# Where the keys of an adjacency tile are shifted: from VectorE to ScalarE, three steps ahead

## What is computed

```
src = concatenate([_s, _d, loop]);  dst = concatenate([_d, _s, loop])
order = argsort(dst);  src = src[order];  dst = dst[order]

def gin_conv(x, src, dst, eps, W1, ln_g, ln_b, W2):
    agg = segment_sum(x[src], dst, num_segments=n)
    h = (1.0 + eps) * x + agg
    h = relu(layer_norm(h @ W1, ln_g, ln_b))
    return h @ W2

xn = layernorm(x)
x = x + gnn_0(xn, edge_index) + mix_0(xn)
x = x + ffn_0(layernorm(x))
xn = layernorm(x)
x = x + gnn_1(xn, edge_index) + mix_1(xn)
x = x + ffn_1(layernorm(x))
```

## Time and profile before

| | us |
|---|---|
| median of 3 runs | 2361.12 (2360.05 to 2365.64) |
| the profiled execution's own time | 2366.88 |
| its span, first to last instruction | 2365.1 |
| the stage of `build_adjacency`, first compare to last | 155.0 to 473.2 |

### The profile page before, as it was taken

One profiled execution on the slowest core, in us unless ns is written; L12 is line 12 of the kernel. 1 busy time (PEld: TensorE's weight loads), 2 busy tenths in 40 slices (PEclk: granted clock), 3 DMA queues, 4 the chain that ended last, 5 costly groups with the idle time before them and its releaser, 6 DMA issues. The chain is left out here.

```text
span 2365.1 us, 41463 instructions
## 1 busy us (share of the span) xinstructions
PE 1997.1 (84%) x12047; PEld 1624.9 (69%) x12047; DVE 1474.2 (62%) x3791; ACT 1036.3 (44%) x1835; POOL 551.5 (23%) x612
## 2 busy tenths in 40 slices
PE   6938888878877758998697898769999965999998
PEld 3526666656633447998365776569888854999997
DVE  3479999978832655554565322399999656444443
ACT  3525555545511524665351343166666430333332
POOL 1000000047611734554310000000000001454443
PEclk9979999977898559999798999989999956999999
DMA  2014334330077301221502342212121081633332
GB/s 69 0 46 133 117 121 129 109 93 1 1 168 211 103 25 54 71 71 54 127 0 54 95 136 63 56 42 65 53 66 53 0 291 54 195 79 75 49 47 33
DMA packets 90653, 189.74 MB, mean 80 GB/s; under 512 B 14121, under 2 KB 58432, under 8 KB 90570
## 3 DMA queue, kind: packets, MB, share of 16 engines
q1 hardware_dynamic: 72906, 157.31, 23.0%
q0 software_dynamic: 17664, 31.47, 6.4%
HBM read 124.22 MB, written 64.52 MB: 80 GB/s over the span
## 5 line engine op out<-in xcount | busy, mean ns | idle before, releaser
L2224 PEld LDWEIGHTS experts_ps_h<-experts_xt,experts_up 128*128 128x128 f32 x2944 | 351.8, 194 | 10.3 <-issue 3.3
L2224 PE MATMUL experts_ps_h<-experts_xt,experts_up 128*128 128x128 f32 x2944 | 353.0, 277 | 3.0 <-DVE experts_xt L2346 1.8
L2851 PE MATMUL gat_ps_o<-Y,gat_prob_t 125*125 125x256 f32 x1250 | 273.9, 379 | 0.0
L2851 PEld LDWEIGHTS gat_ps_o<-Y,gat_prob_t 125*125 125x125 f32 x1250 | 232.7, 188 | 33.7
L1233 PE MATMUL adj_ps_w<-adj_one_k,adj_one_s 128*125 128x500 bf16 x1000 | 178.8, 305 | 78.6 <-DVE adj_one_k L1164 56.0
L2236 PE MATMUL experts_ps_o<-experts_down,experts_hid 128*128 128x256 f32 x960 | 226.7, 379 | 0.0
L2284 ACT ACTIVATE experts_down<-down 128x1024 f32 (+1 forms) x120 | 138.8, 1157 | 175.7 <-DVE experts_out L2334 77.1
L2316 DVE COPY experts_up<-up 128x1024 f32 (+1 forms) x184 | 123.1, 698 | 112.8 <-issue 68.8
L1233 PEld LDWEIGHTS adj_ps_w<-adj_one_k,adj_one_s 128*125 128x125 bf16 x1000 | 98.3, 138 | 128.6 <-DVE adj_one_k L1164 60.2
L2236 PEld LDWEIGHTS experts_ps_o<-experts_down,experts_hid 128*128 128x128 f32 x960 | 173.2, 190 | 18.7
L1177 ACT ACTIVATE adj_tile<-adj_ps_w 125x500 bf16<-125x500 f32 x250 | 95.8, 438 | 150.1 <-PE adj_ps_w L1233 150.1
(11 more groups left out here) (436 smaller groups left out, 3783.9 us busy)
## 6 DMA issues: line engine op xcount, KB each, us to landing
adjacency<-adj_tile SPq DMA_DIRECT2D x25, 683.6 KB
adjacency_t<-adj_tile_t SPq DMA_DIRECT2D x25, 683.6 KB
adj_in<-adjacency_t SPq DMA_DIRECT2D x25, 683.6 KB
QT<-adjacency SPq DMA_DIRECT2D x25, 683.6 KB
cnt<-adjacency_t SPq DMA_DIRECT2D x25, 683.6 KB
up<-in_L_ffn_w SPq DMA_DIRECT2D x32, 512.0 KB, 6.3
down<-in_L_ffn_w SPq DMA_DIRECT2D x16, 512.0 KB, 7.1
up<-in_L_ffn_W SPq DMA_DIRECT2D x8, 512.0 KB, 6.2
```

The source lines that it names most:

```text
L2224: last = nc.tensor.matmul(ps[:, h * 128:(h + 1) * 128], w[:, k * H + h * 128:k * H + (h + 1) * 128], xt[b][:, k, :], start=(k == 0), stop= ...
L2851: last = nc.tensor.matmul(ps_o[b][0:ROWS, 0:C], prob_t[:, s * ROWS:(s + 1) * ROWS], K.Y[:, s, :], start=(s == 0), stop=(s == TILES - 1))
```

## The change

ScalarE makes `key_here`. After the copies of each step it loads the first chunk of the step three ahead from `table` into a register and runs one activation (identity with a bias) that adds the negative of that step's first key (`win_neg`, a new table of GpSimd) to the keys of the four chunks. The first three are made before its first copy. `key_here` has five buffers in place of two, one for each step of a tile. VectorE's instruction goes; its compares still wait for `keyed`, which ScalarE now raises. `table` has three further entries, zero, for the steps beyond the last, ahead of the number of further chunks.

```
-        table = m.sb("table", (1, WINS + 1), I32)
+        table = m.sb("table", (1, WINS + 4), I32)
-        win_key = m.sb("win_key", (CH, WINS))
+        win_key, win_neg = m.sb("win_key", (CH, WINS)), m.sb("win_neg", (CH, WINS + 3))
-        key_here = [m.sb(f"key_here{i}", (CH, FIXED)) for i in range(2)]
+        key_here = [m.sb(f"key_here{w}", (CH, FIXED)) for w in range(WPT)]
...
+            nc.gpsimd.iota(win_neg[:], [[-WIN * TILES, WINS + 3]], base=0, channel_multiplier=0,
+                           allow_small_or_imprecise_dtypes=True)
...
-            v.tensor_copy(table[:, WINS:WINS + 1], most_chunks[:]).then_inc(table_ready, 1)
+            v.memset(table[:, WINS:WINS + 3], 0)
+            v.tensor_copy(table[:, WINS + 3:WINS + 4], most_chunks[:]).then_inc(table_ready, 1)
...
                     dve.wait_ge(win_done, win + 1 + START)
-                    v.tensor_scalar(key_here[half][:], key_all[:, bass.ds(first, FIXED)],
-                                    win_key[:, bass.ds(win, 1)], None, ALU.subtract).then_inc(keyed, 1)
                     v.tensor_tensor(one_s[half][:], K.number_row[:, None, 0:ROWS].to_broadcast((CH, FIXED, ROWS)),
...
                     dve.wait_ge(keyed, win + 1 + START)
                     for j in range(FIXED):
-                        v.tensor_scalar(one_k[half][:, j, :], key_row[:], key_here[half][:, j:j + 1], None,
+                        v.tensor_scalar(one_k[half][:, j, :], key_row[:], key_here[w][:, j:j + 1], None,
                                         ALU.is_equal).then_inc(one_ready, 1)
...
+            def keys(t, w):
+                win = t * WPT + w
+                first = act.value_load(table[:, bass.ds(win, 1)], min_val=0, max_val=CHUNKS)
+                nc.scalar.activation(key_here[w][:], key_all[:, bass.ds(first, FIXED)], ACT.Identity,
+                                     bias=win_neg[:, bass.ds(win, 1)]).then_inc(keyed, 1)
+
             def window(t, b, w):
...
                 last.then_inc(win_read, 1)
+                if w < 2:
+                    keys(t, w + 3)
+                else:
+                    keys(t + 1, w - 2)
...
+            act.wait_ge(table_ready, 1 + START)
+            for w in range(3):
+                keys(0, w)
             for w in range(WPT):
                 window(0, 0, w)
```

More of the change, by code:

```diff
@@ L1140, in _ @@
             dve.drain()
-            v.tensor_copy(table[:, WINS:WINS + 1], most_chunks[:]).then_inc(table_ready, 1)
+            v.memset(table[:, WINS:WINS + 3], 0)
+            v.tensor_copy(table[:, WINS + 3:WINS + 4], most_chunks[:]).then_inc(table_ready, 1)
             dve.wait_ge(table_ready, 1 + START)
-            more = dve.value_load(table[:, WINS:WINS + 1], min_val=1, max_val=MORE_MAX)
+            more = dve.value_load(table[:, WINS + 3:WINS + 4], min_val=1, max_val=MORE_MAX)
             def tile(t, b, i):
@@ L1228, in _ @@
             pe.wait_ge(table_ready, 1 + START)
-            more = pe.value_load(table[:, WINS:WINS + 1], min_val=1, max_val=MORE_MAX)
+            more = pe.value_load(table[:, WINS + 3:WINS + 4], min_val=1, max_val=MORE_MAX)
             def add(banks, ones, keys, start, stop):
```

## The result

The change takes 2337.72 us (median of 4 runs, 2335.93 to 2338.82), against 2361.78 for the kernel before in the same series: a ratio of 0.9892, with a 95% interval of 0.9875 to 0.9910. It is 24 us faster, three times what was forecast, and lies under the range. The profiled execution took 2337.41 us, its span is 2335.7.

A forecast was written before the change was run, and what follows sets the result against it. VectorE was taken as the bound. 24 tiles at 0.32 us give 7.7; with the first tile's 0.65, less 0.1, 8.2 us come off 2361.1: 2352.9, rounded to 2353, range 2345 to 2362.

The forecast's parts named there:

- The bound before: In the changed stage VectorE was taken as nearly full, busy 115.48 of 120 us, with ScalarE half idle.
- The subtraction's 0.13 per step: Taking the subtraction off VectorE saves 0.13 us per step, 0.65 per tile; an undisturbed stride falls from 2.41 to 2.28.
- The load: VectorE's register load of the coming step's chunk stays behind `one_s`, meets the stores' DMA elsewhere; 0.20 of 0.65 per tile left.
- 0.35 + 0.1 per tile: Losses in us claimed for a tile's two long register loads on VectorE, first and second, each growing under a store.
- the subtraction's 16.3 us: Rival: the whole saving on VectorE comes through, 0.65 by 25 tiles, 16.3 us, giving 2345; chance 0.17.
- the prediction's own signs of being wrong: Loads staying short, calm stride not falling, or TensorE's wait for ScalarE well above 0.94 and for VectorE gone.
- The length of the first long load: VectorE's load after a tile's first store starts 0.39 us earlier, becomes 1.2 us long, losing 0.35 per tile.
- The second load: VectorE's load after a tile's other store comes 0.17 us earlier, grows to 1.37, losing 0.04 to 0.14, taken as 0.1.
- ScalarE's part: Load and activation per step are free in the mean, but delay the copy after the fourth step's by 0.3 us.
- The rival in which ScalarE makes the kernel slower: ScalarE's load holds the fifth copy, the TensorE and ScalarE ring passes 12.83; a 2.0 us load gives 2373.6; chance 0.08.
- VectorE's new period still decides: VectorE's period per tile, 12.83 - 0.32 = 12.51 us, stays above the 12.2 of TensorE with ScalarE.
- their ring: TensorE's cycle with ScalarE per tile: 12.83 - 0.93 = 11.90 us, with 0.3 of delay 12.2.

The follow-up runs named there:

- e5_parity_before: The kernel before, with the PSUM set chosen by the step's running number instead of its place in the tile: 2363.46 us, ratio 1.0003.
- e2_both: The change with VectorE's subtraction and its wait put back, ScalarE still making keys that nothing reads: 2363.11 us, ratio 1.0000 to the kernel before.
- e9_own_wait: The change, with each step's first compare also waiting for the count VectorE's own `more_k` raises, no engine work added: 2349.32 us, ratio 0.9937 to the kernel before.
- e6_parity_after: The change, with the PSUM set chosen by the step's running number: 2331.49 us, ratio 0.9863 to the kernel before.
- e4_noload: The kernel before, without VectorE's register loads for the second and third step of each tile (counts wrong): 2350.13 us, ratio 0.9943.
- e10_early_sub: The kernel before, with VectorE's subtraction moved ahead of `more_s` instead of behind `more_k`: 2360.69 us, ratio 0.9981.
- e3_ahead: The change, with ScalarE's key behind the fourth step's copies issued ahead of them: 2334.49 us, ratio 0.9892 to the kernel before.
- e8_spare_sub: The change, with VectorE also subtracting into a tile nobody reads, without a semaphore: 2353.67 us, ratio 0.9968 to the kernel before.

## Why the prediction was wrong

**The bound before: right.** VectorE set the pace (`e5_parity_before`, `e2_both`).

**The subtraction's 0.13 per step: right.** The calm stride was forecast at 2.28 and is 2.28.

**The load: this step failed.** "The stride from `one_s` to the next `more_s` keeps its parts, the load among them." The load's start, 0.26 us after `one_s`, was taken for a fixed part of the step. It was the effect of the wait that the subtraction carried, and it went with it. `e9_own_wait` puts a wait back and gets the forecast's case: two long strides per tile, a period of 12.4 in the mean where 12.51 was forecast. So 0.35 + 0.1 per tile were booked as lost on top of the 0.65 that the loads cost before, and instead that 0.65 left the path too: where VectorE sets the pace its lead covers the first load (`e6_parity_after`), where it doesn't the loss lies beside TensorE's wait, and the second load is short. No case was priced with the loads cheaper than before (a second load ahead of the reading was named, but without the 0.53 us that it saves), so the lower end of the range was the subtraction's 16.3 us; `e4_noload` measures what was missing there, 15.4 us of the stage. Of the prediction's own signs of being wrong the last came: TensorE's wait for VectorE's compares is gone, and that for ScalarE's copies rose, to 1.14.

The length of the first long load came out as forecast (1.2 us; 1.12 to 1.17 from the sixth tile on), but by luck. The load was to start 1.6 us after the store's issue and to end 2.85 after it, where the DMA's reading was thought to end. In the tile shown it starts 1.1 us after the issue at 294.02 and ends 2.2 after it, while the DMA engines read on (share 0.91 in 296.40 to 297.00, below). The assumed end held where the load starts later: 304.64 is the issue in `e10_early_sub`, and the load from 306.1 ends 2.8 us after it.

The second load was to reach 1.37 us. In the change, from the sixth tile to the last but one, it takes 0.30 in every other tile and 0.62 to 1.04 in the rest, for two reasons. VectorE is further ahead of the second store than was thought: the load starts 0.8 us after the issue instead of 1.6, which alone makes it 0.63 to 1.10 (`e3_ahead`). And where ScalarE's late copy holds the store back by a further 0.35 us, the load starts some 0.4 us after the issue and is short; the load of the fourth step then takes 0.6 to 0.7 us and costs nothing. The second effect was named in the prediction, at 0 to 0.5 per tile, and taken at 0.12.

**ScalarE's part: mechanism right, sizes off.** The fifth copy is late behind the key, in the five tiles shown by 0.04 to 0.07 us in one and 0.33 to 0.35 in the next (the waits less 0.94), 0.2 in the mean against 0.3 forecast. The activation of 128x4 takes 0.30 us, not 0.2:

```profile
L1175 ACT ACTIVATE adj_key_here<-adj_key,adj_win_neg 128x4 f32 x128 | 38.3, 299 | 67.0 <-issue 38.5 <-DVE adj_table L1144 28.4
```

The rival in which ScalarE makes the kernel slower needed loads over 1.48 us; the longest is 1.396.

**"VectorE's new period still decides": wrong,** and it follows from the load. TensorE and ScalarE decide, at 11.79; their ring was forecast at 12.2. Of the 0.4 between, 0.3 was TensorE's time at the third step, counted as its own where it had followed VectorE's compares, and 0.1 is ScalarE's smaller delay.

## What to carry to other kernels

A wait on an engine's own earlier instruction can be a wait of its sequencer, as it was here: look at what stands behind it (a register load, an address) and at whether the start of that follows the wait. When an edit takes such a wait away, give the work behind it a case in which it becomes free, not only those in which it stays or grows. And once the bound moves, try again what was worth nothing: the choice of PSUM banks gave 0 before and 6 us of the stage after.

## What the runs showed of the hardware

A register load from SBUF takes 0.27 to 0.3 us with the DMA engines at rest and mostly 0.6 to 1.4 us while they read SBUF (up to 1.62 in `e8_spare_sub`), on VectorE and on ScalarE alike. The windows view of the change for the time of the 1.135 us load and for what comes after its end:

```profile
295.00:296.20 1.20, 0.99 (x8) 0.54 (x6) 1.20 (x4) 0.71 (x4) 0.63 (x2) 1.00 1.02 292
...
296.40:297.00 0.60, 0.00 (x0) 0.01 (x1) 0.40 (x3) 0.47 (x2) 0.00 (x0) 1.00 0.91 323
```

The DMA's share is 1.02 during the load. The Trainium skill's rule of two separate sides ("SBUF — State Buffer", "SBUF: two separate sides"), by which transfers leave the engines' access alone, is again not borne out for these loads; whether they reach SBUF by the engines' side at all, the runs don't show.

What had not been expected is how a wait acts on the instructions behind it. The Trainium skill ("Perfetto Trace Analysis", "DVE / Act Engine Instruction (TENSOR_ADD, Activation, etc)") has an instruction wait for its semaphores in a queue of its own, while the sequencer goes on to the next. The runs agree only in part: in `e6_parity_after`, where the count is up early, the load starts 0.3 us ahead of `one_s`, but in the kernel before and in `e9_own_wait` it starts some 0.25 and 0.45 us behind it, with a wait on the first of the four compares ahead. What it follows is the end of the awaited instruction. In the kernel before the subtraction of 302.43 ends at 302.65, and the load behind it starts at 302.8:

```profile
L1148 DVEq TENSOR_LOAD <-adj_table x1: 305/305/305, 302.8 to 302.8; - x1
```

From the sixth tile on no load of the kernel before starts ahead of that end, and most start about 0.15 us after it; in `e8_spare_sub`, where nothing waits for the same subtraction, loads start up to 1.2 us ahead of it. Why the sequencer does not get past the waiting compare, the runs don't show.
